# A triangle update with its output norm folded into the projection, and an involution whose shifted copies are made partly in place

## What is computed

```python
def _tri_mul(z, ..., outgoing):            # z = z + tm(z, 0, True); z = z + tm(z, 1, False)
    x = _ln(z, lnw, lnb)
    a = sigmoid(x @ agw + agb) * (x @ apw + apb)
    b = sigmoid(x @ bgw + bgb) * (x @ bpw + bpb)
    t = jnp.einsum(eq, a, b)               # the triangle product, over k, per channel
    t = _ln(t, lnow, lnob) @ zw + zb
    return t * sigmoid(x @ gw + gb)
```

```python
kern = (relu(bn(x @ w1 + b1)) @ w2 + b2).reshape(B, H, W, 25, G)
out = jnp.einsum('bhwpg,bhwpng->bhwng', kern, patches)
```

## Time and profile before

| | us |
|---|---|
| median of 3 runs (230.23 to 233.89) | 230.5 |
| the profiled execution | 230.79 |
| its span, first to last instruction | 228.9 |
| PE busy | 209.7 (92%) |
| DVE busy | 141.2 (62%) |
| ACT busy | 128.9 (56%) |
| POOL busy | 90.3 (39%) |

### The profile page before, as it was taken

One profiled execution on the slowest core, in us unless ns is written; L12 is line 12 of the kernel. 1 busy time (PEld: TensorE's weight loads), 2 busy tenths in 40 slices (PEclk: granted clock), 3 DMA queues, 4 the chain that ended last, 5 costly groups with the idle time before them and its releaser, 6 DMA issues.

```text
span 228.9 us, 6522 instructions
## 1 busy us (share of the span) xinstructions
PE 209.7 (92%) x2764; PEld 112.0 (49%) x2764; DVE 141.2 (62%) x253; ACT 128.9 (56%) x218; POOL 90.3 (39%) x103
## 2 busy tenths in 40 slices
PE   7989999979997999989998799998999987899994
PEld 4566743648434544555555454455555522433230
DVE  0443456443687566787786346677768554868881
ACT  2758477846637567755476446775547654215131
POOL 7000000824121143495671004339666500288770
PEclk9999799999999999999999999999999999999999
DMA  6607500222303300000000010000000006950002
GB/s 207 226 6 163 238 0 0 112 79 95 92 1 137 83 0 0 3 3 4 3 3 4 0 37 1 3 0 3 3 3 3 3 0 162 227 100 0 3 0 92
DMA packets 7099, 12.01 MB, mean 52 GB/s; under 512 B 2112, under 2 KB 4032, under 8 KB 6912
## 3 DMA queue, kind: packets, MB, share of 16 engines
q1 hardware_dynamic: 6304, 10.90, 16.1%
q10 hardware_dynamic: 576, 0.70, 0.9%
q0 software_dynamic: 192, 0.00, 0.0%
...
## 4 chain that ended last, share of the span: by engine, by line
PE 74%; DVE 11%; ACT 6%; POOL 3%; issue 3%; DMA 2%; ACTq 0%; DVEq 0%; POOLq 0%
PE psum L1290 7%; PE psum L1233 7%; PE psum L1266 6%; PE psum L1059 5%; PE psum L1441 4%; PE psum L1260 4%; PE psum L1070 4%; PE psum L1459 4%; PE psum L1361 4%; PE psum L1439 4%; PE psum L1150 3%; PE psum L1131 3%; PE psum L1276 2%; PE psum L1337 2%; PE psum L1254 2%
## 5 line engine op out<-in xcount | busy, mean ns | idle before, releaser
L528 POOL TENSOR_TENSOR soft<-soft,rinv 128x512 f32<-128x512 f32 x32 | 33.1, 1042 | 28.2 <-DVE rinv L970 27.7
L711 ACT ACTIVATE soft<-psum 128x512 f32<-128x512 f32 x32 | 19.1, 597 | 22.7 <-PE psum L1290 22.7
L961 DVE TENSOR_REDUCE mx<-psum 128x8 fp32r<-128x512 f32 x32 | 21.5, 683 | 14.3 <-PE psum L1266 14.3
L967 DVE TENSOR_REDUCE rsum<-soft 128x8 f32<-128x512 f32 x32 | 21.5, 671 | 1.0 <-ACT soft L705 1.0
L1290 PE MATMUL psum<-cst,soft 128*128 128x128 f32 x128 | 20.5, 283 | 1.6 <-POOL soft L528 1.2
L1290 PEld LDWEIGHTS psum<-cst,soft 128*128 128x128 f32 x128 | 13.9, 140 | 12.8 <-issue 7.2
L705 ACT ACTIVATE soft<-psum 128x512 f32<-128x512 f32 x32 | 18.6, 595 | 1.0 <-PE psum L1276 1.0
L519 POOL TENSOR_SCALAR gth<-gth 128x512 f32<-128x512 f32 x16 | 9.7, 634 | 22.6 <-ACT gth L698 22.6
L1266 PE MATMUL psum<-Y,x 32*64 32x256 f32 x256 | 17.5, 387 | 0.0
L471 POOL COPY abv<-z1T 128x1024 f32<-128x1024 f32 x1 | 1.9, 1928 | 34.7 <-DVE z1T L895 34.7
L1233 PE MATMUL psum<-x,wyh 128*128 128x512 f32 x32 | 15.3, 612 | 0.0
...
## 6 DMA issues: line engine op xcount, KB each, us to landing
abv<-xhop SPq DMA_DIRECT2D x8, 272.0 KB, 5.2
...
abv<-hop SPq DMA_DIRECT2D x8, 128.0 KB, 2.8
...
```

The lines of the kernel that those rows point to most:

```text
L528: pool.tensor_tensor(PN[u % 2][:, :].rearrange("p (a k) -> p a k", k=N), E_[u % NE][:, :].rearrange("p (a k) -> p a k", k=N), rinv[:, 8 * ...
L711: nc.scalar.activation(PT[u % 2], t_bank(u), ACT.Copy).then_inc(sig(f"{st}_PT"), 1)
L961: nc.vector.tensor_reduce(mx[:, 8 * t:8 * t + 8], bank[t % 4].rearrange("p (a k) -> p a k", k=N), AX_X, ALU.max, negate=True).then_inc(sig ...
L967: nc.vector.tensor_reduce(rsum[:, 8 * u:8 * u + 8], E_[u % NE].rearrange("p (a k) -> p a k", k=N), AX_X, ALU.add).then_inc(sig(f"{st}_sum" ...
```

## The change

- Triangle: the output norm's weight is multiplied into the projection (`wz`), and the centring too (`zoc`, one matmul of 256 columns in tm0, copied by DVE). The projection reads `tB` itself, right after the variances; DVE then multiplies its result by the deviation (`zn`) and applies bias and gate.
- tm0's gate: sigmoid as exp(-ln(1 + exp(-x))) on ACT, with one addition on DVE, in the table set that is loaded. Its norm is finished inside `t_out`, and its two projections stand before and after the transposes. The bias products stand ahead of the triangle.
- `tm1_ln` accumulates on banks 4 and 5, where the centred z0T lies already; `centre_residual` of tm0 is gone, that of tm1 stands ahead of the transposes. The fillers after the triangles are gone.
- The copies to `tP` write runs of 8 neighbouring columns and read PSUM with a stride.
- Involution: the blocks of `xs` that lie on their own partitions are copied by POOL (8 copies); 6 DMAs a half bring the rest. ACT does the first relu before it waits for the second half. POOL also sums the products of units 2 and 3. `ACC_AFTER` is new, and a filler stands ahead of units 3 to 6.

```diff
-        AB_BANKS = ((4, 5, 6, 7), (0, 1, 2, 3))
+        AB_BANKS = (((4, 5, 6, 7), (0, 1, 2, 3)), ((6, 7, 0, 2), (4, 5, 1, 3)))
...
-        ACCUMULATE = [[0], [2], [3], [4]] + [[KS + GB * i + g for g in range(GB)] for i in range(KS)]
-        ACC_AFTER = {5: ((1, 0), (1, 1)), 6: ((2, 0),), 7: ((3, 0),), 9: ((0, 0),), 11: ((0, 1),), 14: ((2, 1), (4, 0)),
-                     17: ((3, 1), (4, 1)), 19: ((5, 0),), 20: ((5, 1),), 23: ((6, 0), (6, 1)), 24: ((7, 0), (7, 1), (8, 0), (8, 1))}
+        ACCUMULATE = [[0], [2], [4]] + [[KS + GB * i + g for g in range(GB)] for i in range(KS)]
+        ACC_AFTER = {6: ((2, 0),), 7: ((2, 1),), 9: ((0, 0),), 10: ((0, 1),), 12: ((1, 0),), 13: ((1, 1),), 15: ((3, 0), (3, 1)),
+                     18: ((4, 0), (4, 1)), 20: ((5, 0),), 21: ((5, 1),), 23: ((6, 0), (6, 1)), 24: ((7, 0), (7, 1))}
         SECOND_HALVES = [n for accs in ACC_AFTER.values() for n, ch in accs if ch == 1]
+        SUMMED = {1: 0, 3: 2}
...
+        def images(t):
+            to = (PAD - SHIFTS[t]) * PW
+            return xs[C * t:C * t + C, to:to + N * PW].rearrange("c (g f) -> c g f", g=GB)
+        OTHER_BLOCKS = ((0, 1, 4), (1, 0, 1), (1, 2, 4), (2, 0, 2), (2, 3, 4), (3, 0, 3))
+        XS_LANDED = 16 * 6
...
+        WARM_UNITS = (3, 4, 5, 6)
         LN = {
             "tm0_ln": (z0R, x, 0, (0, 1), (2, 3), "tm0_lnin", "eps5"),
             "tm0_lng": (z0T, xg, 1, (4, 5), (6, 7), "tm0_lnin", "eps5"),
-            "tm0_lno": (tB, y, 0, (2, 3), (6, 7), "tm0_lnout", "eps5x16"),
-            "tm1_ln": (upd, x, 0, (0, 1), (2, 3), "tm1_lnin", "eps5"),
-            "tm1_lno": (tB, y, 0, (2, 3), (6, 7), "tm1_lnout", "eps5x16"),
-            "ta0_ln": (upd, x, 0, (0, 1), (2, 3), "ta0_ln", "eps5"),
+            "tm0_lno": (tB, None, 0, (1, 3), (1, 3), None, "eps5x16"),
+            "tm1_ln": (upd, x, 0, (4, 5), (1, 3), "tm1_lnin", "eps5"),
+            "tm1_lno": (tB, None, 0, (1, 3), (1, 3), None, "eps5x16"),
+            "ta0_ln": (upd, x, 0, (0, 2), (1, 3), "ta0_ln", "eps5"),
         }
+        GATE_BANKS = (0, 2)
...
-                for t in range(GB):
...
+                for t, g0, g1 in OTHER_BLOCKS:
+                    sp.dma_start(images(t)[:, g0:g1, half_rows(ch)],
+                                 xhop.rearrange("(g c) f -> c g f", c=C)[:, g0:g1, half_rows(ch)]).then_inc(sig(f"xs{ch}"), 16)
...
-            pool.wait_ge(sig("pt_z"), at("pt_z", 2))
+            pool.wait_ge(sig("xs_zero"), at("xs_zero", 2))
+            for ch in range(2):
+                pool.wait_ge(sig("pt_z"), at("pt_z", ch + 1))
+                for t in range(GB):
+                    if ch + t > 0:
+                        pool.wait_ge(sig("xs_own"), GB * ch + t)
+                    pool.tensor_copy(images(t)[:, t, half_rows(ch)], xpad[C * t:C * t + C, half_rows(ch)]).then_inc(sig("xs_own"), 1)
+            pool.wait_ge(sig("xs_own"), 2 * GB)
...
+                    pool.wait_ge(sig("inv_prod_dve"), ON_DVE.index(3) + 1)
+                    pool.tensor_tensor(prod[2], prod[2], prod[3], ALU.add).then_inc(sig("inv_sum"), 1)
...
             def t_out(st):
                 for b in (0, 1):
                     if st == "tm0" and b == 1:
-                        log_variance("tm0_lng", 0)
-                        log_variance("tm0_lng", 1)
+                        deviations("tm0_lng")
                     act.wait_ge(sig(f"{st}_t"), at(f"{st}_t", T_ORDER.index(b) + 1))
-                    nc.scalar.activation(tP[:, :].rearrange("m (n g c) -> m c g n", g=GB, c=C)[:, 8 * b:8 * b + 8],
-                                         bank[b][0:64, :].rearrange("m (c g n) -> m c g n", c=8, g=GB),
+                    nc.scalar.activation(tP[:, :].rearrange("m (n g c) -> m n g c", g=GB, c=C)[:, :, :, 8 * b:8 * b + 8],
+                                         bank[b][0:64, :].rearrange("m (c g n) -> m n g c", c=8, g=GB),
                                          ACT.Copy).then_inc(sig(f"{st}_tP_act"), 1)
+            def gate_exponential(ch):
+                act.wait_ge(sig("tm0_gproj"), at("tm0_gproj", ch + 1))
+                act.wait_ge(sig("neggb"), 1)
+                nc.scalar.activation(half(th, ch), bank[GATE_BANKS[ch]], ACT.Exp, bias=neggb[:, 0:1], scale=-1.0).then_inc(sig("tm0_gexp"), 1)
+            def gate_logarithm(ch):
+                act.wait_ge(sig("gate_sum"), ch + 1)
+                nc.scalar.activation(half(gate, ch), half(gate, ch), ACT.Ln).then_inc(sig("gate_log"), 1)
+            def gate_inverse(ch):
+                act.wait_ge(sig("gate_log"), ch + 1)
+                nc.scalar.activation(half(gate, ch), half(gate, ch), ACT.Exp, scale=-1.0).then_inc(sig("tm0_gate"), 1)
...
             squares("tm0_lng")
             t_out("tm0")
-            for ch in range(2):
-                inverse_deviation("tm0_lng", ch)
+            gate_exponential(0)
             t_back("tm0")
-            layer_norm("tm0_lno", loaded=True)
-            gate_tanh("tm0", 0)
-            layer_norm("tm1_ln")
+            gate_logarithm(0)
+            gate_exponential(1)
+            squares("tm0_lno", (0,))
+            gate_inverse(0)
+            squares("tm0_lno", (1,))
+            gate_logarithm(1)
+            deviations("tm0_lno")
+            gate_inverse(1)
+            layer_norm("tm1_ln", loaded=True)
...
-            act.wait_ge(sig("pt_z"), at("pt_z", 2))
-            act.dma_start(xhop[:, half_rows(1)], xpad[:, half_rows(1)]).then_inc(sig("xhop1"), 16)
             for ch in range(2):
+                if ch == 1:
+                    act.wait_ge(sig("pt_z"), at("pt_z", 2))
+                    act.dma_start(xhop[:, half_rows(1)], xpad[:, half_rows(1)]).then_inc(sig("xhop1"), 16)
                 act.wait_ge(sig("inv_zproj"), at("inv_zproj", ch + 1))
...
+            def scaled_projection(s):
...
+                nc.vector.tensor_scalar(wz[:, 128 * s:128 * s + 128], tmw[:, s * 768 + 640:s * 768 + 768], V(f"tm{s}_lnout_w"), None,
+                                        ALU.mult).then_inc(sig("wz"), 1)
+            def exponential_plus_one(ch):
+                dve.wait_ge(sig("tm0_gexp"), at("tm0_gexp", ch + 1))
+                nc.vector.tensor_scalar(half(gate, ch), half(th, ch), 1.0, 3.0e38, ALU.add, ALU.min).then_inc(sig("gate_sum"), 1)
             def tm_rest(st, s, g, zres, znew, others, weights):
...
                 if st == "tm0":
+                    scaled_projection(0)
                     dve.wait_ge(sig("bias_products"), 1)
                     nc.vector.tensor_tensor(folded[:, :], bank[7][:, 0:3], vec[:, VEC["fold_tm0"]:VEC["fold_tm0"] + 3],
                                             ALU.add).then_inc(sig("folded"), 1)
+                for b in (2, 3):
+                    dve.wait_ge(sig(f"{st}_t"), at(f"{st}_t", T_ORDER.index(b) + 1))
+                    nc.vector.tensor_copy(tP[:, :].rearrange("m (n g c) -> m n g c", g=GB, c=C)[:, :, :, 8 * b:8 * b + 8],
+                                          bank[b][0:64, :].rearrange("m (c g n) -> m n g c", c=8, g=GB)).then_inc(sig(f"{st}_tP_dve"), 1)
+                    if st == "tm0" and b == 2:
+                        scaled_projection(1)
+                        layer_norm("tm0_lng", (0,))
+                if st == "tm0":
+                    dve.wait_ge(sig("zo_product"), 1)
+                    nc.vector.tensor_copy(zoc[:, :], bank[GATE_BANKS[1]][:, 0:256]).then_inc(sig("folded"), 1)
+                    layer_norm("tm0_lng", (1,))
+                    exponential_plus_one(0)
                 dve.wait_ge(sig(f"{st}_ttr"), at(f"{st}_ttr", 2))
                 nc.vector.tensor_copy(sorted_cols(half(tB, 1)), raw_cols(bank[7][:, :])).then_inc(sig(f"{st}_tB_dve"), 1)
                 if st == "tm0":
-                    layer_norm("tm0_lng")
+                    exponential_plus_one(1)
                 weights()
-                layer_norm(f"{st}_lno")
...
-                dve.wait_ge(sig("folded"), 1)
+                dve.wait_ge(sig("folded"), 2)
...
                 for ch in range(2):
                     dve.wait_ge(sig(f"{st}_zo"), at(f"{st}_zo", ch + 1))
-                    nc.vector.scalar_tensor_tensor(half(upd, ch), bank[6 + ch][:, :], folded[:, s:s + 1], half(g, ch),
+                    dve.wait_ge(sig(f"{st}_lno_rstd"), at(f"{st}_lno_rstd", ch + 1))
+                    nc.vector.tensor_tensor(half(y, ch), bank[6 + ch], half(rstd[0], ch), ALU.mult).then_inc(sig(f"{st}_zn"), 1)
+                    dve.wait_ge(sig(f"{st}_zn"), at(f"{st}_zn", ch + 1))
+                    if st == "tm0":
+                        dve.wait_ge(sig("tm0_gate"), ch + 1)
+                    nc.vector.scalar_tensor_tensor(half(upd, ch), half(y, ch), folded[:, s:s + 1], half(g, ch),
                                                    ALU.add, ALU.mult).then_inc(sig(f"{st}_upd"), 1)
...
-            def triangle_back(st, s, in_gap):
+            def triangle_back(st, s):
                 if st == "tm0":
+                    pe.wait_ge(sig("tm0_tP_dve"), at("tm0_tP_dve", 1))
```

(48 more changed lines are left out.)

105 lines of the change are left out of this document (47 added, 58 removed).

## The result

The changed kernel takes 232.3 us (median of 4 runs, 231.9 to 232.5) against 230.4 of the kernel before in the same series (229.3 to 233.9): ratio 1.0096 with a 95% interval of 1.0058 to 1.0133, so slower by about 1%, less than the 2% that the prediction took a measurement to tell. Predicted was 227.9. A median here is of all runs of a kernel, and a ratio leaves out the runs that lie more than 1.5% above the fastest of the same kernel. The profiled execution of the changed kernel took 232.41, with a span of 230.1.

What follows compares the result with a forecast made beforehand. PE held 74% of the chain; the triangle stages were bound by steps between engines, the involution by PE. 230.79 - 3.1 (tm0) - 0.95 (tm1) + 1.4 (involution with hand-over) = 228.1 us profiled, 227.9 median; range 225.2 to 230.3.

Steps and rivals of the forecast that it cites:

- tm0 (-3.1): First triangle stage: folding, gate and copy edits shorten it by 3.1 us, bounds -3.6 and -1.0.
- the fast end of their bounds: Copies to `tP` in tm0: between 0.60 and 1.04 us (DVE 0.69 and 1.02), the fast end taken.
- Rivals 1 and 4: tm0: slow clock returns, 229.4 us; or folding does not shorten it, ACT being the limit, about 229.5; chance together 0.27.
- tm1 (-0.95): Second triangle stage: log of `ta0_ln` starts at 67.55 instead of 68.50 us; -0.95, bounds -1.4 and -0.3.
- Attentions unchanged: Attentions between triangle and involution: nothing touches them, so their length should not change.
- The hand-over (-0.4): Start of the involution: DVE's last split ends at 196.0 instead of 196.38 us, -0.4.
- The involution: Last stage: less accumulation but half the cover of the last product; +1.4 us with the hand-over, bounds -0.6 and +2.4.
- rival 2: Involution: PE stays the only limit and late products are covered, -0.6 instead of +1.4, 225.9 us; chance 0.25.
- The four fillers cost nothing: Involution, ahead of units 3 to 6: the fillers fall in PE's waits for DVE and cost nothing.
- The images (202.5, and nothing gained beyond 203): Involution: images land near 202.5 instead of 204.1 us; needed by 203, and earlier gives nothing.
- Rival 3: Involution: images late, 12 DMAs instead of 8 costing by number, landing at 206.7; +3.7, so 231.6 us; chance 0.06.

Runs made afterwards that it cites:

- e10: Kernel before with the involution part of the change alone, triangle stages as before: 234.6 us, ratio 1.017.
- e2: Changed kernel with the old order and number of accumulations, without POOL's second sum and the four fillers: 227.2 us, ratio 0.989.
- e6: Changed kernel with five fillers between unit 24's kernel and the last accumulation: 232.2 us, ratio 1.008.
- e3: Changed kernel with all images brought by four DMAs a half and no copies on POOL: 240.9 us, ratio 1.046.
- e5: Changed kernel with POOL's four copies of the second half held until DVE's split is done: 231.0 us, ratio 1.003.
- e13: Changed kernel with only the list of accumulations edited, to that of e8: 227.7 us, ratio 0.987.
- e8: Changed kernel with its second sum and fillers, but accumulations in the old list's places (four halves behind unit 24), and two waits on POOL: 228.1 us, ratio 0.987.
- e4: Changed kernel without the fillers ahead of units 3 to 6: 240.2 us, ratio 1.042.
- e12: e9 without the filler ahead of unit 5: 227.2 us, ratio 0.988.
- e1: Kernel before with the triangle part of the change alone, involution and hand-over as before: 233.4 us, ratio 1.015.
- e14: e8 with two and two fillers ahead of the first attention: 227.0 us, ratio 0.985.
- e9: e8 with four and four fillers in two waits of PE ahead of the first attention: 227.0 us, ratio 0.986.

## Why the prediction was wrong, step by step

- **tm0 (-3.1)** came out at -3.06, with the copies to `tP` at 0.59 (ACT) and 0.68 (DVE), the fast end of their bounds, the second update at 34.66 for 34.75, and full clock where the earlier trace rows had 0.57. Rivals 1 and 4 did not come. About 1.4 of it is the half clock, which an execution of the old stages lacked too (e10). The rule of the Trainium skill (SBUF — State Buffer, Door 1: The DMA port swizzle) on accesses within one 16-byte line agrees with the copies: 0.59 and 0.68 us in runs of 8 columns, 1.04 and 1.02 before.
- **tm1 (-0.95)** hit -0.94 by luck. From the start of tm1's triangle the forecast had 16.16 us to the log of `ta0_ln` (67.55 - 51.39) where 17.11 stood; it was 16.85. The steps from the transposes on were written too short: `zn` starts 11.90 us behind the triangle's start, for 11.41, and the second update 14.02, for 13.51. The missing 0.7 came from ahead of the triangle (10.84 to 10.16), most of it from the idle of PE that comes and goes (1.29 to 0.75).
- **"Attentions unchanged"** held in e2 and e6, which have the same code there (119.5 and 119.4 us against 119.4). In the profile of the change 0.9 us were lost, because the bias landed late from DRAM and DVE's split of it then lay beside POOL's additions.
- **The hand-over (-0.4)** was +0.26: the term left the split at its old length (0.42 and 0.75) and asked of POOL's copies only whether they end in time, not what they do to an engine beside them. e3, e5 and e13 show the cause: 0.43 and 0.75 without copies beside it, 0.81 and 1.00 with them.
- **The involution is the term that failed**: with the hand-over in it, +1.4 in the sum and +4.3 in the profiles; of its own from the last split, +1.8 and +4.0. The mechanism was right: the halved cover behind unit 24, the late first accumulation, more and smaller groups. Its size was off: kernels of units 22 and 23 at 24.9 us after the split for 24.3, then 8.5 for 6.75. Of that 1.15 is the half clock at the end, a cost that the sum put at nothing. e13 puts the list of accumulations at 4.65 us of stage time, that half clock included, and 4.6 us of the median: by itself more than the whole miss of 4.4. With the list of e8 the stage is 0.7 shorter than before, about rival 2's figure.
- **"The four fillers cost nothing"** was the step argued least. They cost 0.9 us of delay ahead of unit 6 and hold the clock for 20 us behind it; the prediction looked for the clock in tm0 alone. The medians of e4 and the change lie 7.9 us apart.
- **The images (202.5, and nothing gained beyond 203).** The landing was right: 202.5 is 14.6 us behind the first update of the transition's result in the trace of before. In the changed kernel unit 6 had its image by 14.95 at the latest (199.72 - 184.77); where DVE waited for it, it came at 14.5 (e4, e12) and 15.4 (e5). What was not seen is what the old way costs once the stages move: the price of DMA images was taken from the one trace of before, in which the second half's copy got ahead. e1 and e3 show 6.5 us for that copy, and images at 18.8. Rival 3 had the place and the sign (late images go through to the end), but by the number of DMAs; and it fell on the kernel without the POOL copies, not with them. Its price of +3.7 leaves out the half clock that follows: e3 lies 8.5 above the change.
- **Rule and row:** the Trainium skill (GPSIMD Engine Reference, Engine selection) speaks against two-input arithmetic on POOL. Here the second sum is not what costs: e13 keeps it and its stage is 0.7 us shorter than that of e2 without it (28.7 and 29.4), though the medians (227.7 and 227.2) show no gain.

What stays open: why one bias transfer took 3.6 to 4.0 us in three profiles and 2.5 in others; what the idle ahead of tm1's triangle is; why SP's third image held the queue 1.91 us in the kernel before and not in e1; why the clock falls at 68 us in some runs and not in others of one kernel, which fillers in PE's waits there made rarer (one of six runs in e14, four of six in e8), but e9 moved to 124 us in one run; and the last 0.4 us outside the span.
